# Half tiles at the ends of chunks, another order of the start-up, and another place of the tail's weight copies in a gated cross-attention with routed experts

## What is computed

```python
xn, ln = layernorm(ctx, gm, bm), layernorm(layernorm(x), gl, bl)
q = ln @ Wq + bq;  k, v = split(concat([xn, ln]) @ Wkv + bkv)
attn = softmax(q * DH**-0.5 @ k.T) per head
x = x + tanh(g_xattn) * ((attn @ v) @ Wo + bo)
r = layernorm(x);  p = softmax(r @ Wr + br)
cw = p where in the top 2 of 8, else 0
y_e = relu(r @ W1[e] + b1[e]) @ W2[e] + b2[e]        # hidden width 256
x = x + tanh(g_ffn) * sum_e cw[:, e] * y_e
```

## Time and profile before

| what | before |
|---|---|
| median of three runs | 812.92 us |
| the profiled execution | 810.86 us |
| its span in the trace | 809.1 us |
| TensorE busy with matmuls | 762.6 us, 94% of the span |
| VectorE | 546.2 us, 68% |
| ScalarE | 500.4 us, 62% |
| GpSimd | 445.4 us, 55% |
| bytes moved by DMA | 121.53 MB |

### The profile page before, as it was taken

How to read it: one execution, slowest core, us unless ns; L and a number is a source line. 1 busy time by engine, 2 the same in 40 slices (tenths; PEclk the granted TensorE clock), 3 DMA queues, 4 the chain that set the end, 5 groups by cost and what they waited for, 6 DMA issues and landing times.

```text
span 809.1 us, 17546 instructions
## 1 busy us (share of the span) xinstructions
PE 762.6 (94%) x5418; PEld 647.6 (80%) x5418; DVE 546.2 (68%) x1841; ACT 500.4 (62%) x1631; POOL 445.4 (55%) x454
## 2 busy tenths in 40 slices
PE   4899999998999999999999999999999999979887
PEld 4778777777888988778988878898877898968765
DVE  4637686685858568687758777776869556565445
ACT  2677677676766566766666666656667665555522
POOL 2234264636553544685655586665478566566662
PEclk9999999999999999999999999999999999999999
DMA  5845151532454542175764227574315556534522
GB/s 137 219 185 196 60 206 69 209 143 80 133 195 151 204 165 70 35 237 169 214 207 140 61 74 239 185 234 150 118 56 163 183 179 217 189 105 136 142 70 84
DMA packets 121551, 121.53 MB, mean 150 GB/s; under 512 B 14681, under 2 KB 95858, under 8 KB 121458
## 3 DMA queue, kind: packets, MB, share of 16 engines
q1 hardware_dynamic: 111890, 102.56, 38.8%
q0 software_dynamic: 7680, 15.74, 6.6%
q10 hardware_dynamic: 1888, 2.10, 0.9%
HBM read 36.34 MB, written 41.94 MB: 97 GB/s over the span
## 4 chain that ended last, share of the span: by engine, by line
PE 76%; DVE 7%; issue 6%; POOL 6%; ACT 3%; DMA 1%; ACTq 0%; SPq 0%; DVEq 0%; POOLq 0%
PE shared L1365 13%; PE batch L1303 11%; PE batch L1316 10%; PE hid_ps L1239 8%; PE xy_ps L1253 7%; PE batch L1311 6%; PE shared L1165 3%; PE shared L1167 3%; PE shared L1166 3%; PE batch L1253 2%; POOL probs L650 2%; PE xy_ps L1216 2%; ACT probs L716 2%; POOL yg L640 2%; PE batch L1293 2%
## 5 line engine op out<-in xcount | busy, mean ns | idle before, releaser
L650 POOL TENSOR_TENSOR probs<-probs,rsums 128x512 f32<-128x512 f32 x128 | 133.1, 1040 | 237.7 <-DVE rsums L1096 236.8
L716 ACT ACTIVATE probs<-batch,neg_max 128x128 f32<-128x128 f32 x512 | 180.8, 374 | 3.7 <-DVE neg_max L1100 3.7
L625 POOL DMA_INDIRECT sorted_x<-xn,row_of x120 | 124.7, 1039 | 33.6 <-issue 28.8
L797 ACT ACTIVATE qT<-shared,tb 128x512 f32<-128x512 f32 x128 | 87.3, 697 | 86.0 <-PE shared L1167 73.2
L1303 PE MATMUL batch<-kvT,qT 128*128 128x128 f32 x1024 | 136.3, 276 | 0.8 <-ACT qT L797 0.8
L1316 PE MATMUL batch<-pT_sb,kvn 128*128 128x512 f32 x256 | 133.2, 602 | 2.8 <-ACT pT_sb L724 2.7
L1303 PEld LDWEIGHTS batch<-kvT,qT 128*128 128x128 f32 x1024 | 125.2, 193 | 1.2 <-ACT qT L797 1.2
L1365 PE MATMUL shared<-M,oT 128*128 128x128 f32 x1024 | 125.4, 276 | 0.2
L1365 PEld LDWEIGHTS shared<-M,oT 128*128 128x128 f32 x1024 | 119.4, 192 | 1.4 <-issue 1.3
L716 ACT ACTIVATION_READ_ACCUMULATOR probs<-batch,neg_max 128x1 f32 x512 | 110.0, 215 | 0.0
L1096 DVE RECIPROCAL rsums<-sums 128x4 f32<-128x4 f32 x128 | 22.6, 177 | 123.7 <-ACT probs L716 115.3
(11 more groups left out here) (166 smaller groups left out, 1265.7 us busy)
## 6 DMA issues: line engine op xcount, KB each, us to landing
wt<-wall SPq DMA_DIRECT2D x128, 321.0 KB
sorted_x<-yg SPq DMA_DIRECT2D x36, 512.0 KB, 4.9
xt<-sorted_x SPq DMA_DIRECT2D x168, 64.0 KB
sorted_y<-y_sb SPq DMA_DIRECT2D x84, 128.0 KB
kv<-in_ctx_dram SPq DMA_DIRECT2D x16, 256.0 KB
kv<-in_x_dram SPq DMA_DIRECT2D x16, 256.0 KB
xres<-in_x_dram SPq DMA_DIRECT2D x32, 128.0 KB
out_dram<-x SPq DMA_DIRECT2D x16, 256.0 KB
```

Source lines behind the costliest of these rows:

```text
L625: nc.gpsimd.indirect_dma_start(xs[k % SETS][:, :], bass.IndirectOffsetOnAxis(ap=row_of[:, g, choice, c:c + 1], axis=0), xn[:, g % 2, c, :] ...
L650: nc.gpsimd.tensor_tensor(pv, pv, rsums[:, m % 2, :].unsqueeze(2).broadcast_to([P, 4, P]), ALU.mult).then_inc(probs_ready, 1)
L716: last = nc.scalar.activation(probs[:, m % 2, c * P:(c + 1) * P], batch_ps[m % BANKS][:, c * P:(c + 1) * P], ACT.Exp, bias=neg_max[:, m % ...
L797: nc.scalar.activation(qT[:, g % 2, :, number, :], sh[:, :].rearrange("p (b i) -> p b i", b=GB), ACT.Identity, bias=tb[:, number:number + ...
```

## The change

1. **Half tiles.** `PARTS` gives each tile one or two halves: the last tile of each chunk (15, 31, 47, 63, 75, 83) has one. Loads, weights, turned rows, hidden layer, output and store do only that one.
2. **Start-up.** The second three weight loads are SyncE's, behind its small loads. `every` is a copy by ScalarE instead of a fill by GpSimd, and the mask made of it comes last on GpSimd. Folds use four banks. VectorE normalises all of group 0 before it keeps the first fold.
3. **Normalising.** Where a slot normalises two pairs, both are scaled, then both shifted.
4. **Homes.** The five operations that compute `home` leave `list_tiles` (slot 1 of a group) for `find_homes` (slot 4: slots 36, 60, 84, 108, 124, 132).
5. **The tail's weight copies.** ScalarE fetches the weights of the tile two slots on, behind the next tile's turned rows, instead of the next tile's ahead of them.

```diff
+PARTS = tuple(min(2, HALVES[k] - 2 * t) for k in range(NCH) for t in range(TILES[k]))
...
+MIX = {}
...
+HOMES = 4
...
+        fold_ps, FB = batch_ps, BANKS
...
+                    load_weights(sp, 1)
...
-                for a in range(2):
+                for a in range(PARTS[i]):
...
-            for half in range(2):
-                if half == 1:
-                    act.wait_ge(got_kv, 32)
...
+            load_weights(act, 0)
+            act.wait_ge(const_step, 4)
+            nc.scalar.activation(every[:, :], ones_sq[:, :], ACT.Copy).then_inc(every_ready, 1)
...
-                if TILE_AT.get(n + 1, 0) >= LATE:
-                    fetch_weights(TILE_AT[n + 1])
                 if n + 1 in TILE_AT:
...
+                if TILE_AT.get(n + 2, 0) >= LATE:
+                    fetch_weights(TILE_AT[n + 2])
...
+                if n == FOLD_FROM:
+                    for k in range(4):
+                        scale_kv(0, k)
+                    for k in range(4):
+                        shift_kv(0, k)
+                        if k in MIX:
+                            keep_folded(MIX[k])
...
+            def normalise_kv(n):
+                ks = [k for k in range(4) if (n - NORMALISE[k]) % GB == 0 and 0 < (n - NORMALISE[k]) // GB < G]
+                for k in ks:
+                    scale_kv((n - NORMALISE[k]) // GB, k)
+                for k in ks:
+                    shift_kv((n - NORMALISE[k]) // GB, k)
...
+            def find_homes(n, s):
+
+                g = n // GB - 2
+                if s == HOMES and g in LAST_GROUP:
+                    k = CHUNK_OF_GROUP[g]
                     nc.vector.tensor_scalar(gap[:, :], n_tiles[:, 0:E - 1], -float(HALF), float(ROWS), ALU.mult, ALU.add).then_inc(table_step, 1)
...
                 list_tiles(n, s)
+                find_homes(n, s)
```

More of the change, by code:

```diff
@@ L361, in flamingo @@
         const_step = sem("const_step")
+        every_ready = sem("every_ready")
         gates_done = sem("gates_done")
@@ L447, in shared_at, with halves_to @@
                     if places[-1] == place and (what in on_dve) == (reader == "dve")]
+        def halves_to(i, step):
+            return sum(PARTS[j] for j in range(i % step, i + 1, step))
         def wait_tiles_read(eng, k):
             for b in range(XB):
-                wait(eng, got_x[b], 32 * len(range(b, FIRST_TILE[k + 1], XB)))
+                wait(eng, got_x[b], 16 * sum(PARTS[j] for j in range(b, FIRST_TILE[k + 1], XB)))
         def wait_rows_scattered(eng, k):
@@ L602, in _ @@
                                     base=0, pattern=[[1, E], [-1, E]], channel_multiplier=0).then_inc(const_step, 1)
-            nc.gpsimd.affine_select(out=earlier[:, :], in_=every[:, :], compare_op=ALU.is_gt, fill=0.0,
-                                    base=0, pattern=[[1, P]], channel_multiplier=-1).then_inc(const_step, 1)
             nc.gpsimd.iota(first_row[:, :], [[ROWS, E]], base=0, channel_multiplier=0,
@@ L614, in _ @@
                            allow_small_or_imprecise_dtypes=True).then_inc(const_step, 1)
+            pool.wait_ge(every_ready, 1)
+            nc.gpsimd.affine_select(out=earlier[:, :], in_=every[:, :], compare_op=ALU.is_gt, fill=0.0,
+                                    base=0, pattern=[[1, P]], channel_multiplier=-1).then_inc(const_step, 1)
             def scatter_rows(g, c):
@@ new lines, in scale_kv, with shift_kv @@
+            def scale_kv(g, k):
+                for b in (2 * k, 2 * k + 1):
+                    last = nc.vector.scalar_tensor_tensor(out=kv[:, b, :], in0=kv[:, b, :], scalar=mv[:, b, 0:1],
+                                                          in1=gamma[:, :], op0=ALU.subtract, op1=ALU.mult)
+                last.then_inc(kv_scaled, 1)
+            def shift_kv(g, k):
+                if k == 0:
+                    dve.wait_ge(rstd_done, g + 1)
+                dve.wait_ge(kv_scaled, 4 * g + k + 1)
+                wait(dve, o_ready, GB * g + 2 * k + 2 - KVN)
+                for b in (2 * k, 2 * k + 1):
+                    last = nc.vector.scalar_tensor_tensor(out=kvn[:, (GB * g + b) % KVN, :], in0=kv[:, b, :], scalar=rstd[:, b:b + 1],
+                                                          in1=beta[:, :], op0=ALU.mult, op1=ALU.add)
+                last.then_inc(kv_ready, 1)
@@ L1125, in slot @@
                 aggregate_kv(n, s)
-                if n != FOLD_FROM:
-                    for k in range(4):
-                        normalise_kv(n, k)
+                normalise_kv(n)
                 read_logits(n, s)
@@ L1189, in weights @@
                         turn_weights(h + 1)
-                    fold = batch_ps[h % 2]
-                    if h >= 2:
-                        pe.wait_ge(w_lo, h - 1)
+                    fold = fold_ps[h % FB]
+                    wait(pe, w_lo, h - FB + 1)
                     pe.wait_ge(w_copied, h + 1)
```

70 lines of the change are left out of this document (29 added, 41 removed).

## The result

The changed kernel takes **803.16 us** (median of four runs, 801.74 to 804.18; the kernel before 812.87 beside it), a ratio of 0.9887 (95% interval 0.9875 to 0.9899). The forecast was 802.5 with a range of 799 to 808. The sum was right; several of its terms were not. The tail gave 2 to 3 us less than forecast; homes and pairing gave more, and on average the start-up too. That the number came out so close is partly luck. (One slip in the description: `HALF` is 128 rows, so a half has 128 rows and a tile 256. No number hangs on it.)

A forecast was written before the change was run, and what follows sets the result against it. TensorE, busy 94% of the span, bounds the saturated middle; in the tail waits count, and the start-up saturates nothing. Seven terms sum to 10.4 us off the 812.92 median: 802.5 us, 8-in-10 range 799 to 808.

The forecast's parts named there:

- Start-up, -1.8: Before the first query: earlier function table load and folds, and VectorE normalising first, save 1.8 us; bounds 0.8 to 2.2.
- TensorE's fold chain ... is not the later strand: In the start-up: TensorE's folds come earlier by about as much as VectorE's 1.4 us, so they do not set the pace.
- Pairing, -1.0: Later groups' normalising: eight waits of TensorE for turning `kvn` shrink by 0.12 us each, 1.0 us; bounds 0 and 1.9.
- Homes, -0.3: Homes moved to slot 4: 1.26 us saved in slot 34, 0.95 lost in slots 36, 60, 84, 108; net 0.3 saved.
- In the later chunks TensorE had tile work there and no wait: nothing: Homes leaving slot 1 in chunks after slot 34's save no time, as TensorE did not wait there.
- The bound of +1.4: Unfavourable end of the homes term: 0.9 us longer in slot 36 and 0.5 in each of the three other slots.
- Half tiles, -3.0: Tiles 15, 31 and 47, where TensorE is saturated: each lost half saves 1.0 us, 3.0 together; bounds 2.4 and 3.3.
- The tail, -4.25: After attention: 1.15 us saved by tile 66, 1.7 around `prob`, 1.4 for tiles 75 and 83.
- The first rival: The tail gives nothing, because an unexplained delay holds it; saving 6.15 us, time 806.8; chance 0.21.
- the second rival: The tail gives more: without the 2.66 us wait TensorE may stay at 2.4 GHz; saving 12.8 us, 800.1; chance 0.12.

The follow-up runs named there:

- the experiment: The changed kernel with the homes computed in slot 1 of a group again, against the changed kernel at 802.9 us: 803.99 us.

## Why the prediction was right, and where its steps were not

- **Start-up, -1.8: near in size, half right in kind.** Landing to slot 0 went from 22.4 to 20.6, and to 18.9 to 20.7 over ten traces with this start-up. What I missed is that scaling no longer waits for `rstd`; it would have made VectorE's strand 1.4 us shorter again, had TensorE's folds not become the later one. "TensorE's fold chain ... is not the later strand" is wrong, and with it the start-up now hangs on when TensorE's clock rises, which the sum did not consider.
- **Pairing, -1.0: measured -1.4 by the slots, 0.9 by the medians.** Not eight times 0.12: slot 1 alone has 0.6, most others 0.06. Where the wait for `kvn` shrank, the next wait took most of it, as the prediction feared: in slot 65 it fell from 0.62 to 0.37 us, that for GpSimd's probabilities rose from 0.67 to 0.83.
- **Homes, -0.3: measured -0.9.** What leaves slot 34 (1.26 by the experiment) and what arrives in slot 36 (0.74 against 0.8) were right. Two sizes were wrong: slots 60, 84 and 108 cost 0.29 each, not 0.05. Two things add up there: the half tile took away their cover, an interaction that I costed at nothing (with whole tiles they cost nothing), and `gap` stands 0.48 us longer beside GpSimd's multiply, which I had counted in slot 36 alone. The two were not undone apart, but the read-out would come 0.48 earlier without the second; and "In the later chunks TensorE had tile work there and no wait: nothing" missed 0.54 us in slot 122 and 0.8 in slots 59, 83 and 107 together. The bound of +1.4 does not follow from the numbers given for it: 0.9 + 1.5 - 1.26 is 1.1.
- **Half tiles, -3.0: right**, 1.00 in slots 57 to 59, before the homes take 0.29 back in slot 60.
- **The tail, -4.25: the step that failed.** Slot 127 to the end went from 115.9 and 116.1 to 114.7 and 113.9, 1.2 to 2.2 us (113.4 to 115.3 over eight traces of the changed kernel and its variants, leaving out the faster set and the run without gathers); undoing the half tiles or the copies' place loses none of it (114.2, 113.4). What gave this 1 to 2 us is open. The first rival had this ("the time taken from ScalarE, VectorE and TensorE there turns into waiting"), and had the cause as the delay without a name. I took waits with a named releaser (`xtT`, `hs`) for causes, where those engines were themselves waiting for TensorE's late signals. Its total, 806.8, was wrong because the rest gave more than I had summed.
- **The clock**: the second rival's way, a tail without half clock, did not come about: the eight hidden matmuls behind the wait of 2.12 us take 2.08 us where eight take 1.06 at 712.76 (from 717.1 to 723.9 the granted clock is 0.50), and the granted clock of the stretch from 712 to 764 is 0.90; at the lower level were 10.2 us of the tail, 6.8 and 10.2 in the two traces of before.
- **The sum.** By the traces: 1.8 + 0.6 + 4.4 (631.2 and 630.4 to 626.4, the middle) + 1.7 = 8.5 us. By the medians 9.7 to 10.0. With the average of nine traces for the way to slot 8 the first two terms are 2.9 and the sum is 9.0. Undoing parts one by one gives 1.8 + 1.1 + 0.9 + 1.5 + 3.3 + 0.9 = 9.5; of these the first 0.9, that of the copies, is not clear of the scatter. What is left between traces and medians lies in landings and tail, of which two traces each are too few.

## What to carry to other kernels

Before work is moved to a place where it fits "just so", ask what the same change takes away next to it, and what runs beside it: 0.18 us of slack in slot 60 was gone with half a tile's output and a wait of 0.48 beside GpSimd's multiply. When several engines stand idle at once and each names another as releaser, compare the recorded end of the work with the rise of its semaphore: a gap of microseconds there tells that the named engines were not the bound, and here taking work from TensorE and ScalarE gave nothing. When one strand of a start-up becomes TensorE's, look at the pace of its first matmuls: here the moment at which its clock rose made 1.8 us between executions of the same start-up. And undo every part of a change by itself: the place of the copies was worth nothing that could be measured, the banks and the order of the folds 3.3 us.

## What the runs showed of the hardware that was not expected

- TensorE's semaphores rose 1 to 2 us after the recorded end of its work on average, up to 5, several within 0.15 us (718.81, 718.90, 718.95 in the kernel after), while GpSimd issued indirect gathers one after another (0.95 us each). Without these gathers the tail is 14 us shorter. Scatters may do it too: they alone were under way where signals were 2 to 3 us late in that run. How gathers delay the signals is open: through the DMA traffic that they make or through something on GpSimd's side was not tried.
- The same kernels, in another set, had almost no lateness with the gathers in place, and the kernel before took 795.09 us instead of 812. For the changed kernels the stretch from y65 to y83 accounts for most of it (40.9 against 54 us). It was another chip; whether the chip is the reason was not tried.
- A VectorE operation on 7 columns with one input took 0.64 us instead of 0.16 when it was issued during GpSimd's multiply, and ended 0.03 us after it, in slots 36, 60, 84 and 108 alike.
- The first folds ran at the lower level of TensorE's clock until 4 to 9 us after the rows had landed, and the moment differed between executions by 4.7 us, which moved slot 0 by up to 1.8 us.
